# A graph network on one core: the attention stage reordered (norms by half, unit strides in the last group, an early exponential table)

## The reference

```python
# layer 0: three matmuls with gelu over the edges, segment sum, norm, three matmuls over the nodes, norm
h = layer_norm(h_V + dh, ln1_g, ln1_b)
d = gelu(gelu(h @ d0_w + d0_b) @ d1_w + d1_b) @ d2_w + d2_b
y = layer_norm(h + d, ln2_g, ln2_b)
x = layernorm(x + y)                               # "xp" in the kernel
# layer 1: attention among the 8 heads of ONE node
Q, K, V = [(x @ W).reshape(N, 8, 32) for W in (Wq, Wk, Wv)]
score = softmax(einsum('nhd,ngd->nhg', Q, K) / sqrt(32))
x1 = einsum('nhg,ngd->nhd', score, V).reshape(N, 256)
attn_out = segment_sum(x1[dst] * x1[src], dst)     # = x1 * (count @ x1)
h = layernorm(x + attn_out @ O_w + O_b) ...        # then an FFN, a norm, a GRU and the last norm
```

## Time and profile before

| | us |
|---|---|
| median of 3 runs | 637.98 (633.39 to 640.4) |
| the profiled execution, its time | 636.32 |
| the profiled execution, its span | 634.6 |
| PE busy | 595.0 (94%) |
| DVE busy | 459.5 (72%) |
| ACT busy | 365.0 (58%) |
| granted TensorE clock, mean | 0.988 |

### The profile page before, as it was taken

How to read it: one execution, slowest core, us unless ns; L and a number is a source line. 1 busy time by engine, 2 the same in 40 slices (tenths; PEclk the granted TensorE clock), 3 DMA queues, 4 the chain that set the end, 5 groups by cost and what they waited for, 6 DMA issues and landing times.

```text
span 634.6 us, 9167 instructions
## 1 busy us (share of the span) xinstructions
PE 595.0 (94%) x3281; PEld 510.0 (80%) x3281; DVE 459.5 (72%) x777; ACT 365.0 (58%) x551; POOL 189.2 (30%) x179
## 2 busy tenths in 40 slices
PE   4999998999999999999999989987999999887994
PEld 2888887988898888888888878877988888676752
DVE  5746586777788878788877868798465466798646
ACT  4577686767776767776777756653183431211331
POOL 3044354345434554355534534400000001000100
PEclk9999999999999999999999989999899999999998
DMA  7994399397499479649639983331000514000000
GB/s 250 307 280 142 138 270 305 117 279 269 147 262 290 142 220 305 185 156 286 192 131 267 431 297 111 94 83 43 1 2 0 208 34 200 0 1 1 0 1 33
DMA packets 51483, 102.82 MB, mean 162 GB/s; under 512 B 3568, under 2 KB 41328, under 8 KB 46960
## 3 DMA queue, kind: packets, MB, share of 16 engines
q1 hardware_dynamic: 45104, 86.04, 44.1%
q0 software_dynamic: 5760, 15.92, 7.7%
q10 hardware_dynamic: 576, 0.28, 0.2%
HBM read 66.69 MB, written 35.53 MB: 161 GB/s over the span
## 4 chain that ended last, share of the span: by engine, by line
PE 78%; DMA 9%; DVE 7%; issue 2%; ACT 2%; POOL 1%; SPq 0%; POOLq 0%; DVEq 0%; ACTq 0%
PE ps L1191 24%; PE ps L1227 8%; DMA sorted_raw<-sorted_rows 7%; PE ps L1373 7%; PE ps L1233 4%; PE ps L1209 4%; PE ps L1205 4%; PE ps L1204 4%; PE ps L1341 3%; PE ps L1272 3%; PE ps L1276 3%; PE ps L1274 3%; PE ps L1384 2%; PE ps L1299 1%; PE ps L1411 1%
## 5 line engine op out<-in xcount | busy, mean ns | idle before, releaser
L452 POOL DMA_INDIRECT sorted_rows<-m,place x120 | 163.1, 1359 | 214.7 <-ACT m L514 186.2
L771 DVE TENSOR_TENSOR m_lo<-m_out,m_hi 128x512 fp32r<-128x512 f32 x128 | 88.8, 694 | 60.4 <-ACT m_out L499 57.0
L497 ACT ACTIVATE m_hi<-ps,cols 128x512 fp32r<-128x512 f32 x128 | 88.5, 691 | 75.5 <-PE ps L1191 47.5
L1191 PE MATMUL ps<-x_lo,w_hi 128*128 128x512 f32 x256 | 100.7, 393 | 0.0
L1191 PE MATMUL ps<-x_hi,w_hi 128*128 128x512 f32 x256 | 100.6, 393 | 0.0
L1191 PE MATMUL ps<-x_hi,w_lo 128*128 128x512 f32 x256 | 100.5, 392 | 0.0
L499 ACT ACTIVATE m_out<-ps,cols 128x512 f32<-128x512 f32 x128 | 88.1, 688 | 0.0
L687 DVE TENSOR_TENSOR x_lo<-x_raw,x_hi 128x1024 fp32r<-128x1024 f32 x64 | 75.7, 1223 | 7.4 <-ACT x_hi L491 7.4
L1227 PE MATMUL ps<-w_lo,m_hi 128*128 128x256 f32 x256 | 64.2, 283 | 0.0
L1227 PE MATMUL ps<-w_hi,m_hi 128*128 128x256 f32 x256 | 64.0, 282 | 0.0
L491 ACT ACTIVATE x_hi<-x_raw 128x1024 fp32r<-128x1024 f32 x62 | 62.3, 1059 | 1.8 <-DMA x_raw<-in_edges_dram 1.8
(11 more groups left out here) (206 smaller groups left out, 1141.0 us busy)
## 6 DMA issues: line engine op xcount, KB each, us to landing
x_raw<-in_edges_dram SPq DMA_DIRECT2D x31, 1024.0 KB, 7.5
sorted_raw<-sorted_rows SPq DMA_DIRECT2D x24, 647.5 KB, 6.2
sorted_rows<-no_edge SPq DMA_DIRECT2D x6, 2460.5 KB, 19.3
d_w<-in_d_dram SPq DMA_DIRECT2D x1, 4096.0 KB, 26.6
sorted_rows<-no_edge SPq DMA_DIRECT2D x2, 1942.5 KB, 17.6
sorted_raw<-sorted_rows SPq DMA_DIRECT2D x6, 518.0 KB, 4.2
rows<-in_rows_dram SPq DMA_DIRECT2D x1, 2176.0 KB, 8.8
d_w<-in_d_dram SPq DMA_DIRECT2D x2, 1024.0 KB, 13.9
```

Source lines behind the costliest of these rows:

```text
L452: pool.indirect_dma_start(out=sorted_d, out_offset=bass.IndirectOffsetOnAxis(ap=place[:, at:at + 1], axis=0), in_=m2[:, b % 2, t], in_offs ...
L497: nc.scalar.activation(out_hi[:, m], ps[:, bank], ACT.Gelu, bias=col(bias, m)).then_inc(hi_signal, 1)
L771: nc.vector.tensor_tensor(lo[:, m], m_out[:, m], hi[:, m].bitcast(F32), ALU.subtract).then_inc(done, 1)
L1191: last = nc.tensor.matmul(out, left, right, start=(k == 0 and i == 0), stop=(k == KE - 1 and i == 2))
```

## The change

Four things are done.

1. Each half is normed by itself: half 0's second `moments` and its xp stand before half 1's first sums, and half 1's last `moments` and its xp stand in the attention part, xp behind the first score product. POOL's calls follow.
2. The order on DVE: `w_rz` and `b_gru` go from in front of the first score product to behind group 3's score product; both `skip` sums go in front of the first `scores`; group 3's reduce, softmax and output come behind group 2's. `score_products` waits for Q and K of its group only, and `out_products` for V. ACT's order is adapted.
3. Group 3 uses the weights the other way round: wqk as loaded, and `wv_turned` (a new copy on ACT, [128, 512]). Its products then lie with the summed dimension inside, at unit stride, in all three instructions.
4. A one-column exponential on ACT behind act_T of half 0, so that the table load stands there.

The banks of the output sums are 3, 1, 0 in place of 0, 1, 3, and PE's wait for all Q, K, V copies goes behind the first output sum and group 2's score sum.

```diff
-        SCORE_BANK, OUT_BANK = (2, 6, 2), (0, 1, 3)
+        SCORE_BANK, OUT_BANK = (2, 6, 2), (3, 1, 0)
...
-            inverse_std(NODE_HALF[0])
-            inverse_std(range(NC))
-            inverse_std(NODE_HALF[1])
+            for half in range(2):
+                inverse_std(NODE_HALF[half])
+                inverse_std(NODE_HALF[half])
...
             affine(0, None, None)
+            nc.scalar.activation(top[:, 0:1], cols[:, 0:1], ACT.Exp, scale=0.0)
             qkv(0)
             qkv(1)
+            nc.scalar.activation(wv_turned[:].rearrange("p k (d g) -> p k d g", g=HEADS),
+                                 wv[:].rearrange("p k (g d) -> p k d g", g=HEADS), ACT.Copy).then_inc(wv_ready, 1)
             affine(1, None, None)
...
             sums_out(0, 3)
-            exponential(3, 3)
-            exponential(2, 4)
+            exponential(2, 3)
             sums_out(1, 5)
+            exponential(3, 4)
             sums_out(2, 6)
...
             between_norms(NODE_HALF[0])
+            moments(NODE_HALF[0])
+            hats_written(0, lambda c: normed(res, xp, c))
             sums_and_stats(NODE_HALF[1], d2_done, product_rows, skip)
-            moments(range(NC))
-            hats_written(0, lambda c: normed(res, xp, c))
+            moments(NODE_HALF[1])
             between_norms(NODE_HALF[1])
-            moments(NODE_HALF[1])
-            hats_written(1, lambda c: normed(res, xp, c))
...
-                dve.wait_ge(qkv_out, 2 * c + 2)
+                dve.wait_ge(qkv_out, 2 * c + 1)
...
-            link(nc.vector.tensor_reduce(probs[:, 3].rearrange("p h g -> p (h g)"),
-                                         prod[3].rearrange("p (d r) -> p r d", d=DH), AX_X, ALU.add))
+            link(nc.vector.tensor_reduce(probs[:, 3], view, AX_X, ALU.add))
...
-            v = v_rows[:, 3].rearrange("p (a g d) -> p a d g", a=1, g=HEADS).to_broadcast([P, HEADS, DH, HEADS])
+            v = v_rows[:, 3].rearrange("p (a d g) -> p a d g", a=1, g=HEADS).to_broadcast([P, HEADS, DH, HEADS])
...
+                qk_w, v_w = (wqk, wv_turned) if c == NC - 1 else (wqk_turned, wv)
...
-            pe.wait_ge(qkv_out, 2 * NC)
             add_up(0, OUT_BANK[0])
             add_up(2, SCORE_BANK[2])
+            pe.wait_ge(qkv_out, 2 * NC)
             add_up(1, OUT_BANK[1])
```

More of the change, by code:

```diff
@@ L225, in gnn_kernel @@
         wqk_turned = sb("wqk_turned", [P, KH, 2 * H])
+        wv_turned = sb("wv_turned", [P, KH, H])
         prod = (prod01[:, 0], prod01[:, 1], prod2[:], f1_T[:].rearrange("p k n -> p (k n)"))
@@ L317, in gnn_kernel @@
         rz_weights = sem("rz_weights")
-        wqk_ready = sem("wqk_ready")
+        wqk_ready, wv_ready = sem("wqk_ready"), sem("wv_ready")
         bias_sums, b_hi_done, b_split = sem("bias_sums"), sem("b_hi_done"), sem("b_split")
@@ L1076, in out_products @@
             def out_products(c):
+                dve.wait_ge(qkv_out, 2 * c + 2)
                 sm = probs[:, c].rearrange("p h (g a) -> p g h a", a=1).to_broadcast(pairs)
@@ L1084, in _ @@
             dve.wait_ge(d2_done, NC)
+            moments(NODE_HALF[1])
+            score_products(0).then_inc(prod_ready, 1)
+            hats_written(1, lambda c: normed(res, xp, c))
+            score_products(1).then_inc(prod_ready, 1)
+            for half in range(2):
+                dve.wait_ge(hat_ready, hats[0] - 2 + 2 * half)
+                cs = slice(2 * half, 2 * half + 2)
+                nc.vector.tensor_tensor(skip[:, cs], xp[:, cs], row_half(row("O_b")), ALU.add)
+            for c in range(2):
+                scores(c, c + 1)
+                less_top(c)
+                softmax(c, c + 1)
+                if c == 0:
+                    out_products(c)
+            score_products(2).then_inc(prod_ready, 1)
+            out_products(1)
+            dve.wait_ge(qkv_out, 2 * NC)
+            q = qk_rows[:, 3, 0:H].rearrange("p (h a d) -> p h a d", h=HEADS, a=1).to_broadcast(pairs)
+            k = qk_rows[:, 3, H:2 * H].rearrange("p (a g d) -> p a g d", a=1, g=HEADS).to_broadcast(pairs)
+            view = prod[3].rearrange("p (h g d) -> p h g d", h=HEADS, g=HEADS)
+            link(nc.vector.tensor_tensor(view, q, k, ALU.mult))
             nc.vector.tensor_tensor(w_rz[:], w_ih[:, :, 0:2 * H], w_hh[:, :, 0:2 * H], ALU.add).then_inc(rz_weights, 1)
@@ L1090, in _ @@
             nc.vector.tensor_copy(b_gru[one, 3 * H:4 * H], hh[:, 2 * H:3 * H]).then_inc(bias_sums, 1)
[L1091 to L1102, removed]
-            link(nc.vector.tensor_reduce(probs[:, 3].rearrange("p h g -> p (h g)"),
-                                         prod[3].rearrange("p (d r) -> p r d", d=DH), AX_X, ALU.add))
-            less_top(3)
-            softmax(3, 3)
             scores(2, 4)
             less_top(2)
-            softmax(2, 4)
+            softmax(2, 3)
             out_products(2)
-            dve.wait_ge(hat_ready, hats[0])
-            nc.vector.tensor_tensor(skip[:, 2:4], xp[:, 2:4], row_half(row("O_b")), ALU.add)
+            link(nc.vector.tensor_reduce(probs[:, 3], view, AX_X, ALU.add))
+            less_top(3)
+            softmax(3, 4)
             sm = probs[:, 3].rearrange("p h (a g) -> p h a g", a=1).to_broadcast([P, HEADS, DH, HEADS])
-            v = v_rows[:, 3].rearrange("p (a g d) -> p a d g", a=1, g=HEADS).to_broadcast([P, HEADS, DH, HEADS])
+            v = v_rows[:, 3].rearrange("p (a d g) -> p a d g", a=1, g=HEADS).to_broadcast([P, HEADS, DH, HEADS])
             view = prod[3].rearrange("p (h d g) -> p h d g", h=HEADS, d=DH)
@@ L1397, in qkv @@
                     pe.wait_ge(qkv_out, 2 * c - 2)
-                for bank, weights, width in ((c % 2, wqk_turned, 2 * H), (4 + c % 2, wv, H)):
+                if c == NC - 1:
+                    pe.wait_ge(wv_ready, 1)
+                qk_w, v_w = (wqk, wv_turned) if c == NC - 1 else (wqk_turned, wv)
+                for bank, weights, width in ((c % 2, qk_w, 2 * H), (4 + c % 2, v_w, H)):
                     for k in range(KH):
```

## The result

The changed kernel takes 632.93 us against 638.25 us before, each the median of 20 executions. Their ratio, estimated from the single executions, is 0.9922, with a 95% interval of 0.9902 to 0.9942: 0.8% faster, inside the 1% that the prediction allows for a measurement of this kernel. One execution of the changed kernel, of 1074 us at a mean clock of 0.708, is left out of the ratio.

What follows compares the result with a forecast made beforehand. DVE was taken to bound the stage, then PE, two chains ending together. Terms along DVE summed to -4.4, clocked as -4.5 to -4.6; 4.6 taken from the median 637.98 gave 633.4, forecast 633.2 us, range 629 to 637.9.

Steps and rivals of the forecast that it cites:

- The chain before: Attention stage of the old kernel: chain runs almost wholly through DVE from 542.0 to 572.8 us without a gap, then PE.
- Two chains end together: End of the stage: PE's gathers end 0.17 us after DVE's own work, so a gain counts only if both shorten.
- Norms by half: Start of the stage: norming half 0 alone wins 0.37 us, between 0.21 and 0.57; the other 2.2 are hidden by filler.
- First score product: DVE, group 0: starts when its Q and K are out, at 540.15, 1.88 us earlier than before.
- The table: Group 0's softmax: early table load under PE's Q and K; table and its queue give -1.44 us along DVE.
- sum by causes: Savings and added work along DVE, listed by cause: together -4.4 us, by the step by step clock -4.5 to -4.6.
- The small waits: DVE: new waits of 0.6 us for group 2's Q and K and 0.1 before its scores; PE's rest before first sum 0.3.
- Moved sums hide behind PE: w_rz and b_gru, 2.14 us, behind group 3's score product fill DVE's wait for PE, costing nothing beyond PE's pace.
- Unit strides: Group 3's reduce and output product: 1.39 + 1.45 = 2.84 us saved; new score product between 2.21 and 3.74, taken as 2.21.
- the rival of the dimensions: Group 3's reduce and product: four-dimensional pattern costs, not stride, so 2.84 us stay; gain 1.8, time 636.2; chance 0.07.
- The table rule: ACT: the skill's 1283 ns load plus 1380 ns drain, 2.66 us per switch, weighed against 1.3 us in the trace.
- The clock rival: New order may make PE rest and its clock fall behind the gathers, at most 3.4 us each; chance 0.06, a third slower.

Runs made afterwards that it cites:

- e3: Kernel before with group 3's unit-stride forms alone (wv_turned, exchanged weights), old order: stage 48.87 us against 50.24, ratio 0.9959.
- e5: Changed kernel with half 0's second norm behind half 1's first again, one moments for all groups: stage 46.23 us against 45.69, ratio to before 0.9919.
- e2: Changed kernel without the early one-column exponential, so the table load stands before group 0's exponential: stage 46.18 us against 45.69, ratio to before 0.9874.
- e4: Changed kernel with w_rz and b_gru in front of the first score product again: stage 48.82 us with a clock fall, 47.13 in a second trace without.
- e1: Changed kernel with group 3's old strided forms (wqk_turned and wv, no wv_turned): stage 49.93 us, second trace 49.22, both with a clock fall.
- e10: Kernel before with the early one-column exponential alone, old order: stage 51.04 us with a clock fall, against 50.24; ratio 0.9960.
- e9: e8 with no filler at all: 47.12 us from the last layer-0 matmul against 44.27 in e8, with a clock fall; ratio to before 0.9936.
- e6: Changed kernel with 8 filler products in place of 14 ahead of the first turn: stage 45.02 us against 45.69, ratio to before 0.9928.
- e8: Changed kernel with 8 filler products, first score product before the wait for POOL, ones and b_gru_lo behind the gather's products: stage 44.15 us, ratio to before 0.9925.

## Why the prediction was right

The time was forecast at 633.2 and came at 632.93; the gain forecast was 4.6 us, the stage shows 4.55 and the medians 5.3, with an interval of 3.7 to 6.3 from the ratio. That the time fits to 0.3 us is luck: the forecast set out from a median of three executions, 637.98, single executions scatter by 8 us, and 633.2 is itself 0.2 less than 637.98 - 4.6, without a reason given. What bears the prediction out is the stage. Another reading agrees with it: in the comparisons of the experiments 29 executions of the kernel before had a mean clock of 0.988, and took 637.1 us on average; the nine of the changed kernel at that clock took 632.8, 4.3 less.

*The chain before.* The prediction says that DVE works from 542.0 to 572.8 without a gap. Its own rows have DVE idle for 1.61 and 1.76 us in that stretch, where PE's first sum and ACT's table load stood in the chain. The steps that follow use these waits, so no figure hangs on the sentence.

*Two chains end together.* Shown by e3: with DVE alone shortened, its wait for PE went from 0.17 to 1.51 us and half the gain was lost.

*Norms by half, 0.37 us.* 0.54 in the stage (e5), inside its bounds of 0.21 to 0.57. The 2.2 us of the filler's cover are as foreseen.

*First score product.* Forecast 8.2 us after the filler's start (540.15), measured 8.12. x1 of group 3 was forecast at 575.0; the last reduce ended at 576.23, less the 1.18 of this execution 575.05 (the prediction's terms add up to 574.9, a slip of 0.1). DVE's multiplication was forecast at 576.35 and came at 577.54 - 1.18 = 576.36.

*The table, -1.44 in the sum by causes.* As a share of the chain this term was right only on paper. The wait in group 0 did shrink from 1.76 to 0.32 us, but undoing the edit costs 0.49 (e2): the wait of 0.8 us for Q and K of group 2 would swallow the rest. In this stretch the chain runs through PE, as the chain of the changed kernel shows. The sum came out because that wait stood in it as a term of its own (+0.6). The attribution to causes was too generous, the clocking of one engine after another was not. The same goes for the other terms: taken back one at a time, norms, table, weight sums and strides cost 0.54, 0.49, 1.44 and 2.61 us (the last to x1, without the fall), together 5.1 where the whole change brings 4.55.

*The small waits.* PE's rest before the first sum was forecast at 0.3 us and was 0.50. The new wait for Q and K of group 2: 0.6 forecast, 0.83 measured. The 0.1 before group 2's scores did not come; 0.21 us stand before its output product instead.

*Moved sums hide behind PE.* e4 shows it: in front they cost 1.44 us (47.13 against 45.69), and the wait that they filled is back.

*Unit strides, -2.84.* 2.61 to x1, as measured by e1; the rival of the dimensions is out. The new score product took 2.28, near the lower of its bounds, 2.21.

*The table rule.* The load took 1.28 us, began 0.01 us after the copy before it ended, and had the dummy 0.02 us behind it; undoing the edit lengthens group 0's wait by the same 1.28 us (0.32 to 1.60, e2). The drain of 1380 ns that the Trainium skill, "ScalarE: Activation LUTs", section "What ACT_TABLE_LOAD costs", adds to each switch is not to be seen in these traces.

*The clock rival.* It did not happen in the stage of the changed kernel, but it is real here, and the prediction had its sign too simple. It treated a fall as a risk of the change. Eight traces have a rest of PE of 1.9 us or longer in this stage, and five of them a fall behind it; of the six without such a rest none has a fall there. The changed kernel has no rest of more than 0.94 us there, where the kernel before had 1.93 and 2.35. The change should thus remove an occasional loss of 1.7 us besides its 4.55. This is argued from the variants: the one trace of the kernel before has no fall in the stage, and whether such falls are the difference between 4.55 and the 5.3 of the medians is within the scatter and not shown.

## What to carry to other kernels

Follow one engine's clock through the new order, wait by wait, and not a sum of savings: the same table load was worth 0.9 us in one order (less the fall) and 0.5 in the other, and the same unit strides 1.4 or 2.6. Put work that is due late into the gap where an engine waits for another, and look which of two chains ends second before shortening one. Where PE waits for others, its rest has a price of its own, since the clock may fall in it.

## What the runs showed of the hardware

The scatter of this kernel's times goes with the mean granted clock of the execution. In the 19 executions of the changed kernel that the ratio rests on, by clock: 0.991, 628.31 to 631.27 (4 runs, mean 630.06); 0.988 to 0.989, 631.58 to 634.48 (10 runs, mean 632.8); 0.985, 632.85 to 636.87 (4 runs, mean 634.63); the nineteenth had 0.982 and 636.25. So a good part of the spread of 8 us, which is wider than the whole gain, goes with falls of the clock; about 3 to 4 us are left inside a group. Some of the falls stand at the same place in every trace: read in stretches of 4 us, all fourteen have a clock under 1.00 somewhere from 436 to 448 us of the span. Others come and go: ten have one from 372 to 380, four from 600 to 612, seven from 624 to 628.

A rest of PE of 1.93 to 1.95 us at one place in the program was followed by a fall in two traces and by none in three; rests of 2.69, 3.56 and 3.57 us were each followed by one; rests of 2.35 us (before, ahead of the last output sum), of 1.46 us (e10, the same place), of 1.22 us (e2) and of 0.94 us by none. So the length of the rest alone does not decide. The clock read 0.50 (1.2 GHz) where a whole stretch of 2 us lay in a fall (e4, e9 and e1's second trace), and sixteen matmul passes took 5.41 us where the fall caught them, 3.72 otherwise.

A gap of 0.20 to 0.21 us stands before group 2's output product in the changed kernel, e2, e4, e5 and e6, in both traces where there are two, put down to DVE's own preceding instruction. It is missing before, in e3 and e10, in e1 and in e8 and e9. Its cause is open.
